# Twelve step-size sums of the state-space scan, moved from VectorE to GpSimd

## What is computed

```python
deltaBC = jnp.einsum('bld,od->blo', x, W_bc)
dt = jnp.einsum('blr,dr->bld', dt_r, W_dt)
delta = jax.nn.softplus(dt + b_dt[None, None, :])
# scan over time, for every feature d and state n:
dA = jnp.exp(delta_t[:, :, None] * A[None])
dBu = (delta_t * u_t)[:, :, None] * B_t[:, None, :]
h = dA * h + dBu
y_t = jnp.einsum('bdn,bn->bd', h, C_t)
```

## Time and profile before

| | us |
|---|---|
| median of 3 runs (1906.12 to 1910.46) | 1906.67 |
| the profiled execution, its own time | 1907.46 |
| its span | 1905.7 |
| PE busy | 1771.2 (93%) |
| DVE busy | 1339.0 (70%) |
| POOL busy | 1281.3 (67%) |
| ACT busy | 987.1 (52%) |

### The profile page before, as it was taken

How to read it: one execution, slowest core, us unless ns; L and a number is a source line. 1 busy time by engine, 2 the same in 40 slices (tenths; PEclk the granted TensorE clock), 3 DMA queues, 4 the chain that set the end, 5 groups by cost and what they waited for, 6 DMA issues and landing times. The chain is left out here.

```text
span 1905.7 us, 27715 instructions
## 1 busy us (share of the span) xinstructions
PE 1771.2 (93%) x9472; PEld 1136.7 (60%) x9472; DVE 1339.0 (70%) x1660; ACT 987.1 (52%) x1671; POOL 1281.3 (67%) x992
## 2 busy tenths in 40 slices
PE   7898998898999999889999899998999999999998
PEld 5666666577755565455555555554556555567886
DVE  2525344333259999899897999889999999994222
ACT  5344343566465656655556456555555555543212
POOL 4533444155449998798877898788889898883111
PEclk9999999899999999999999999999999999999999
DMA  7342332587668887688676887676778777874652
GB/s 243 129 144 73 122 110 92 183 298 272 240 217 278 290 294 264 215 299 276 209 251 226 276 278 253 236 238 231 248 256 278 253 254 254 279 261 155 209 190 98
DMA packets 159292, 427.37 MB, mean 224 GB/s; under 512 B 30992, under 2 KB 54160, under 8 KB 158768
## 3 DMA queue, kind: packets, MB, share of 16 engines
q1 hardware_dynamic: 159152, 425.60, 66.2%
HBM read 356.34 MB, written 69.21 MB: 223 GB/s over the span
## 5 line engine op out<-in xcount | busy, mean ns | idle before, releaser
L1627 ACT ACTIVATE decay<-delta_on_states,a_neg 128x512 f32<-128x512 f32 x512 | 353.9, 693 | 351.8 <-DVE h_states L1756 333.5
L1849 POOL TENSOR_TENSOR q_or_raw_or_h_times_c<-h_states,c_rep 128x512 f32<-128x512 f32 x293 | 382.9, 1318 | 63.1 <-DVE h_states L1756 38.0
L1849 POOL TENSOR_TENSOR h_times_c_rest<-h_states,c_rep 128x512 f32<-128x512 f32 x219 | 282.4, 1299 | 47.2 <-DVE h_states L1756 29.8
L1815 POOL TENSOR_TENSOR h_lo<-v_or_silu_in_h_lo,h_hi 128x512 fp32r<-128x512 f32 x128 | 167.0, 1305 | 207.4 <-ACT h_hi L1534 207.0
L1736 DVE TENSOR_TENSOR d_b<-du_spread,b_rep 128x512 f32<-128x512 f32 x384 | 256.4, 668 | 22.5 <-PE du_spread L1457 22.1
L1756 DVE TENSOR_TENSOR_SCAN h_states<-decay,h_last,d_b 128x512 f32<-128x512 f32 x192 | 245.5, 1279 | 12.7 <-ACT decay L1627 5.9
L1457 PE MATMUL du_spread<-stack,selectors 96*128 96x512 bf16 x512 | 201.3, 393 | 49.2 <-DVE d_b L1736 34.2
L1756 DVE TENSOR_TENSOR_SCAN h_states<-decay,d_b 128x512 f32<-128x512 f32 x192 | 233.9, 1218 | 17.5 <-ACT decay L1627 11.3
L111 PE MATMUL y_or_aux<-h_hi,w 128*128 128x512 f32 x468 | 222.2, 475 | 6.6 <-POOL h_lo L1815 4.3
L112 PE MATMUL y_or_aux<-h_lo,w 128*128 128x512 f32 x468 | 184.1, 393 | 0.0
L113 PE MATMUL y_or_aux<-h_hi,w 128*128 128x512 f32 x468 | 183.5, 392 | 0.0
(11 more groups left out here) (251 smaller groups left out, 4205.4 us busy)
## 6 DMA issues: line engine op xcount, KB each, us to landing
delta_on_states<-delta SPq DMA_DIRECT2D x256, 512.0 KB, 5.4
w<-w_split SPq DMA_DIRECT2D x112, 512.0 KB, 4.3
attn_w_hi_or_x_hi_w<-w_split SPq DMA_DIRECT2D x112, 512.0 KB, 4.3
attn_w_lo_or_x_lo_w<-w_split SPq DMA_DIRECT2D x112, 512.0 KB, 4.3
w_split<-w_presplit_hi_lo SPq DMA_DIRECT2D x32, 512.0 KB, 3.3
w_presplit_hi_lo<-in_w13b SPq DMA_DIRECT2D x32, 256.0 KB, 3.8
w_split<-attn_w_hi_or_x_hi_w SPq DMA_DIRECT2D x8, 1024.0 KB, 6.8
w_split<-attn_w_lo_or_x_lo_w SPq DMA_DIRECT2D x8, 1024.0 KB, 7.0
```

What stands on the lines that cost most here:

```text
L1627: act.activation(da[:, s % ND], dring[:, s % NR], ACT.Exp, scale=a[:, column(s):column(s) + 1]).then_inc(s_da, 1)
L1815: pool.tensor_tensor(hl[:, idx % RH], sg[:, idx % RH], hh[:, idx % RH].bitcast(F32), ALU.subtract).then_inc(s_hl, 1)
L1849: pool.tensor_tensor(hc[s % NC_], hs[:, s % NH], crep[:, tile_of(s // SPO) % 2], ALU.mult).then_inc(s_hc, 1)
```

## The change

The sum of relu and logarithm is made by GpSimd for the pieces of the second, third and fourth tile. In its tick, GpSimd makes it behind its product with C, its own input and its low halves (L1815, L1822, L1806), and ahead of the two subtractions of a piece (L1828 and L1832 before) if these fall in the same tick. The same two waits stand ahead of it as before, and it raises the same signal `s_de`. On DVE the sum of the first tile stays.

```diff
--- before.py
+++ after.py
@@ -1785,7 +1785,7 @@
                         centre(e, k)
                     for e, k in SCALE_AT.get(tick, ()):
                         scale(e, k)
-                    if tick in SIZE_AT:
+                    if tick in SIZE_AT and SIZE_AT[tick][0] == 0:
                         step_size(*SIZE_AT[tick])
                     if tick in INPUT_AT:
                         step_input(*INPUT_AT[tick])
@@ -1821,6 +1821,11 @@
                         pool.wait_ge(s_xl, KD)
                     pool.tensor_tensor(xl[:, f % 2, k], x[:, k, tok(f % NT)],
                                        xh[:, f % 2, k].bitcast(F32), ALU.subtract).then_inc(s_xl, 1)
+
+                def step_size(t, m):
+                    pool.wait_ge(s_so, KD * t + m + 1)
+                    pool.wait_ge(*taken("dt", (t, m)))
+                    pool.tensor_tensor(delta_of(t)[:, m], delta_of(t)[:, m], soft_of(t)[:, m], ALU.add).then_inc(s_de, 1)
 
                 def part_rest(t, m):
                     rest = soft_of(t)[:, m]
@@ -1866,6 +1871,8 @@
                         x_low(*SPLIT_AT[tick])
                     if tick - 1 in W2_HIGH_AT:
                         w2_low(W2_HIGH_AT[tick - 1])
+                    if tick in SIZE_AT and SIZE_AT[tick][0]:
+                        step_size(*SIZE_AT[tick])
                     if tick in REST_AT:
                         part_rest(*REST_AT[tick])
                     if tick in LOW_AT:
```

## The result

The changed kernel takes 1913.9 us (11 runs, 1907.58 to 1918.0) against 1906.12 us of the kernel before (11 runs beside it, 1901.35 to 1911.22). The ratio is 1.0041, with an interval from 1.0026 to 1.0056: 7.8 us slower. That lies inside the predicted range, on the side of the two rivals that forecast a loss (0.18 and 0.07). The profiled execution took 1917.79 us, the second slowest of the eleven and 3.9 us above their median, with a span of 1916.0, 10.3 us more than the profiled span before.

A forecast was written before the change was run, and what follows sets the result against it. DVE, 91 to 96% busy, was taken to bound the scan. The profiled 1907.46 us, plus piece lateness (+1.8 - 3.3 + 1.5 = 0.0) and long holds (+1.4), gave 1908.9, or 1908 us in the runs' terms; range 1897 to 1916.

The forecast's parts named there:

- the two rivals that forecast a loss: POOL becomes the pace (0.18), 1915 to 1921.7 us, and SP's queue held at its store (0.07), 1914.5 us.
- The half of the mechanism: On DVE, 13.0 of L1723's 21.3 us are not work: two-input instructions take turns with POOL's, and L1727 loses another turn.
- That DVE sets the pace: Between 700 and 1600 us DVE, 91 to 96% busy, limits the kernel; shortening its queue helps unless POOL takes over.
- The rival of SP's queue: SP's store L1258 waits longer for POOL's sum, delaying loads for decay and DVE: 1914.5 us, 1922 at most; chance 0.07.
- its first rival: DVE gives back all its time, L1727 finding the sum done and POOL between instructions: 1896 us; chance 0.21.
- the last term of the sum: Long holds of DVE at L1727: about one in twelve, worth half of 2.5 us, adding +1.4 us.
- my own case: DVE's gains and losses at the moved pieces cancel, long holds add +1.4: 1908 us, spanning 1902 to 1913; chance 0.54.
- The pieces one by one: When L1727 ends on DVE, by tile: second +1.8 us late, third 3.3 early, fourth +1.5 late after waits absorb 1.0.
- if L1727 is passed over here: At piece (2, 3), L1727 waits for three more POOL instructions, ending at 1093.0: 0.8 us earlier instead of 3.3.
- That DVE gives back all its time: L1727 on DVE finds POOL's sum done and POOL between instructions: 1885 to 1898 us, taken as 1896; chance 0.21.
- That POOL becomes the pace: Twelve added sums on POOL are paid in full, 1921.7 us, or half where gaps swallow some, 1915; chance 0.18.

The follow-up runs named there:

- experiment 2: Kernel before, without the sum for the second to fourth tile on any engine, the store waiting for L1727: 1908.47 us; with the store waiting for the logarithm: 1905.93 us.
- the second version of experiment 2: Kernel before, without the sum for the second to fourth tile on any engine, SP's store waiting for the logarithm instead: 1905.93 us, 1.0003.
- experiment 3: Changed kernel, with POOL waiting behind each moved sum until DVE has done L1727 of the same piece: 1907.87 us, 1.0011.
- Experiment 1: Kernel before, with twelve extra sums of a constant on POOL that nobody waits for, DVE keeping its own sums: 1915.53 us, 1.0046.
- Experiment 6: Changed kernel, with L1727 of the second to fourth tile on POOL as well: 1915.55 us, 1.0042.
- experiment 7: Changed kernel, with ACT's first rounding of a piece (L1615) and POOL's first subtraction one tick later: 1911.57 us, 1.0012.
- experiment 5: Changed kernel, POOL's sums of m = 1 to 3 four ticks earlier: 1910.45 us; with POOL also waiting for L1727 in its tick: 1909.59 us.

## Why the prediction was right, and where it was off

**The half of the mechanism that held.** L1723's excess was waiting for access, not work, and L1727 inherits it, as experiment 2 shows with the sum gone altogether: 16.3 of 21.3 us return. That DVE sets the pace, with which the prediction began, held only in part: what was taken from its two lines came back as waits for ACT and PE in the second version of experiment 2 (5.0 us off, 5.8 on) and in experiment 3 (11.9 us off with the idle time, 11.3 on).

**Sizes that held.** POOL's sum, 1.25 us predicted, is 1.29. POOL's busy time rose by 11.9 us (1293.2 against 1281.3), in 10 to 15. The rival of SP's queue was not seen: its wait is 29.2 us against 29.5, where I had expected more.

**Signs that failed.** DVE was to be busy for about 10 us less, with as much new idle time ahead of L1727. It was busy for 1340.4 us against 1339.0, and the idle time was 3.9 us. The prediction named little idle time as the sign of its first rival, a gain; here it came with a loss, because the wait was inside L1727.

**The step that failed is the last term of the sum**, "the chance of long holds at L1727: 3 in 32 of both lines times twelve is about one, worth half of the 2.5 us": +1.4. Five of twelve took 3.0 us or more, four of them over 4. The term has two faults. I took the chance from both lines together, as if L1723's long stands left with L1723, but the next line inherits them: with no sum anywhere and no more work on POOL, three of twelve L1727 took over 4 us. And I took it from pieces where POOL's backlog was what it was before, while the change adds to that backlog just ahead of L1727. Experiment 1 isolates this: 15 us more on POOL made the unchanged instructions of DVE stand 7.2 us longer. By the signs that the prediction gave, L1727 would have been 1.3 to 1.9 us each, some 19 us, with about 10 us of new idle time, 29 in all; measured were 34.6 and 3.9, 38.5 in all, 9.5 us more.

**The number was partly luck.** The median is 5.9 us above the 1908 predicted, beyond the 1902 to 1913 that my own case spans, and beyond the 0.3% that it was given. It lies in the range because the range was stretched for the rivals.

**The pieces one by one** went wrong with it. The third tile was to be 3.3 us early and is 3.3 late (steps 204 to 240); the second +1.8 and is +5.2; the fourth +1.5 and is +2.0. Pieces (2, 1) to (2, 3), which were to come out early, had long stands at L1727 (3.00, 5.43 and 4.82 us). At (2, 3) this is what the text allowed for ("if L1727 is passed over here"), at the other two it isn't.

**The rivals.** That DVE gives back all its time is refuted for more than this change, by experiment 2: it doesn't even when the sum costs nothing anywhere. That POOL becomes the pace was closest: its time, half of the 15 us, is what was measured. But its sign in the profile is missing. The scan's matmuls on PE waited 1.2 us for POOL's products before and wait 1.2 us now (700 to 1300 us), and POOL still had 48 us idle in each of the first two stretches. POOL's time is paid where an instruction of DVE with two SBUF inputs meets it. Experiment 6, in which DVE has only the norms of that kind between 700 and 1320 us and the loss is the same, shows that this isn't the only way.

The Trainium skill (SBUF — State Buffer, section "SBUF: two separate sides") says of the shared port pair that whoever starts first keeps it for the whole instruction. The trace agrees that they exclude each other. It doesn't bear out what the prediction drew from the page, that a loser waits for the running instruction only (6.68 us behind five).

**What stays open** is what decides, at the end of a POOL instruction, whether DVE gets in. Piece (3, 1), where it did, in the changed kernel:

```profile
1275.65 1.76 DVE L1727 TENSOR_TENSOR soft_in_x_hi<-delta_in_x_lo,x 128x512 f32<-128x512 f32 x1 [1.08 <-POOL delta_in_x_lo L1828]
```

And POOL at the same place:

```profile
1274.32 1.29 POOL L1828 TENSOR_TENSOR delta_in_x_lo<-delta_in_x_lo,soft_in_x_hi 128x512 f32<-128x512 f32 x1
1275.56 2.99 POOL L1854 TENSOR_TENSOR q_or_raw_or_h_times_c<-h_states,c_rep 128x512 f32<-128x512 f32 x2
```

DVE asks 0.09 us behind the start of POOL's L1854, as it did at 817.55 (817.46), with the same line of POOL running and the sum just done. Here it loses one turn and POOL some 0.46 us, there DVE loses five. (Differences under 0.1 us on POOL are rough.) It isn't fixed by the program either: L1723 of piece (0, 2), which the change doesn't touch, took 4.1 us before and 0.8 after. So where a long stand falls looks partly like chance of an execution, and 5 of 12 is no constant. Nor is it settled how much of the loss passes through ACT's queue (experiment 7).

## What to carry to other kernels

Don't count on GpSimd's idle share to hide work moved there from VectorE, if instructions of VectorE with two SBUF inputs run beside it: here whichever of them came next paid for the backlog. Look first at the duration of those instructions against the shortest one of their kind. In this trace what is above it was a wait, and removing one such instruction handed most of its wait to the next. What helped was to make GpSimd wait on the semaphore of the VectorE instruction (experiments 3 and 5), and more, a form of softplus with less work for ScalarE and no sum. Taking the sum off both engines by itself brought nothing (experiment 2), and neither did taking both instructions off VectorE (experiment 6).

## What the runs showed of the hardware

An instruction of DVE with two SBUF inputs, 0.69 us alone, waited in these runs behind the running instruction of POOL and up to five more in a row (6.68 us behind four more here, 6.88 in experiment 1 and 7.24, the longest, in experiment 5 behind five more), and shows as busy all the time.

TensorE's granted clock fell behind such a stand. The columns are those of the earlier trace rows, in the changed kernel around the 5.43 us that L1727 took from 1077.02:

```profile
1080.00:1085.00 5.00, 0.63 (x2) 0.64 (x3) 5.00 (x5) 1.46 (x3) 3.17 (x3) 0.79 0.95 347
1085.00:1090.00 5.00, 5.00 (x16) 1.95 (x16) 4.56 (x5) 3.31 (x6) 4.45 (x4) 0.52 0.49 176
```

PE had nothing to do for most of the first 5 us (0.63 busy). Its matmuls of L1457 wait for DVE's L1736, once for 5.8 us here, and 22.0 us in all between 700 and 1300 us, 16.5 before. In the next five it was granted 0.52, which is near the lower of its two levels (1.2 of 2.4 GHz). It was busy throughout then, yet DVE waited for it only 0.9 us between 1080 and 1120 us. The grant fell behind the 4.82 us of 1098.52 as well (0.68 from 1105 to 1110), and in the kernel before behind the 5.14 us of 1085.56 (0.79 and 0.86 from 1090 to 1100). So here the lower clock looks like a consequence of the stand and hardly a cost of its own; that was read, not tested.
